# A graph network on one core: GpSimd writes 256 elements of a scratch tile behind every second row gather

## The chip, the core and the metric

The kernel runs on one core of one Trainium2 chip (trn2). A time is the device time of one execution in microseconds (us). A kernel is timed in several runs and the median is given. The profile and the trace are of one execution. PE is TensorE, DVE is VectorE, ACT is ScalarE, POOL is GpSimd and SP is SyncE; the last one only issues DMAs here. The granted clock of PE is a share of its full speed: 0.5 is 1.2 GHz and 1.0 is 2.4 GHz.

## The reference

Eight graphs (b) with 1024 nodes and 128 features go through four layers. A residual sum and a layer norm stand behind each of them.

```
x = _layernorm(x + _L0_gnn_ref(adj, x, L0_W, L0_b))                 # sampled neighbours, max
x = _layernorm(x + _L1_gnn_ref(x, adj, L1_W, L1_b, L1_a))           # graph attention
x = _layernorm(x + _L2_gnn_ref(x, adj, L2_W, L2_a))                 # graph attention
x = _layernorm(x + _L3_gnn_ref(x, adj, att_W, W0, b0, W1, b1))      # masked attention, two steps

def _L0_gnn_ref(A, X, W, b):            # the layer that the change is about
    scores = where(A != 0, -arange(N), -inf)
    vals, idx = top_k(scores, 25)       # the first 25 neighbours of every node
    feats = X[idx], where valid, else -inf
    agg = feats.max(axis=2)             # and at least 0 where a node has 25 neighbours or fewer
    return relu(concatenate([X, agg]) @ W + b)
```

## The kernel before, in words

A graph's 1024 nodes are eight tiles t of 128 nodes, one on each partition. Five instruction streams, one for each engine, are written out by hand. They meet at semaphores, and each stream runs its instructions in the order in which they stand. Graph 0 has a start of its own. Then a loop takes two graphs in each pass, and the last two graphs stand behind it.

The 25 neighbours of layer 0 come in two ways. For the first 21 of them (13 in graph 0), DVE lists the rows of x that are wanted (`find_keys`, `find_members`, which ends in `list_rows` at L1171). GpSimd then issues one indirect DMA for each slot k (`gather`, L508). One such gather fetches 128 rows of 512 bytes, one for each partition, into `gathered`, a ring of three tiles. DVE takes the maximum over the slots of a tile (`pool_tile` at L1204 and L1205, for tile 3 in two halves at L1212 and L1217). It then raises `rows_pooled`, which frees the place in the ring. The other slots are picked by matmuls with one-hot matrices (`make_hot` at L1249 on DVE, L563 and L566 on ACT; `pick` at L817 on PE).

All of this is done one graph ahead. While the engines work on graph b, the lists, gathers and picks of graph b+1 are placed between the steps of graph b, by the table `SIDE`. GpSimd does nothing else once its constants are made: it has 8 tiles of 13 gathers and 56 tiles of 21 gathers, 1280 in all. Before each tile it waits for the list of rows (`rows_ready`, for every second tile) and for the free place (`rows_pooled`). In steady state these waits cut a graph's eight tiles into five bursts, of 42, 21, 21, 42 and 42 gathers. Within a burst the gathers follow each other at once. Other lines named below are L917 and L764 on PE (heads of a graph attention layer and the packing of the adjacency bits) and L1277 on DVE (a small step of the layer norm).

Of the kernel before, what the change touches and what calls it, by code (L numbers as in the profile page):

```python
# [11 lines left out]
BF16 = mybir.dt.bfloat16  # L12
# [7 lines left out]
P = 128  # L20
# [9 lines left out]
GATHERED = (21, 21)  # L30
GATHERED_FIRST = 13
LATE = 6
PICKED = (SAMPLES - GATHERED[0], SAMPLES - GATHERED[1])
PICKS = PICKED[0] + PICKED[1]
BY_DVE = (PICKED[0], PICKED[0] + 1)
PICKED_FIRST = SAMPLES - GATHERED_FIRST
# [67 lines left out]
def gathered_up_to(b, t):  # L104

    return sum(gathered_slots(b, i) for i in range(t % RING, t + 1, RING))


def half_and_slot(b, q):
    if isinstance(b, int) and b == 0:  # L110
        return divmod(q, PICKED_FIRST)
    return (0, q) if q < PICKED[0] else (1, q - PICKED[0])

# [7 lines left out]
def late_rows(t):  # L121

    return LATE if t == 7 else 0

# [13 lines left out]
def build_graph_layers(nc, x, adj, w0, b0, w1, b1, a1, w2, a2, watt, w3a, b3a, w3b, b3b, out):  # L138
    B, N, C = x.shape
    T = N // P  # L140
# [12 lines left out]
    with ExitStack() as ctx:  # L153
        def sb(name, shape, dt=F32):
            return ctx.enter_context(nc.sbuf_tensor(name, shape, dt))
# [4 lines left out]
        def signal(name, per, unit=1, ahead=0, first=None):  # L160
            return Signal(ctx, nc, name, per, unit, ahead, first)
# [48 lines left out]
        row_f = sb("row_f", [P, 2, GATHERED[0]])  # L210
        rows = sb("rows", [P, T, GATHERED[0]], U32)
        gathered = sb("gathered", [P, RING, GATHERED[0] * C])
        running = sb("running", [P, T, N // 2], BF16)
        hot = [sb(f"hot{c}", [P, T // CHUNKS, N // 2], F32R) for c in range(CHUNKS)]
        x_parts = [sb(f"x_part{i}", [P, T, C], F32R) for i in range(X_PARTS)]
# [57 lines left out]
        def pick_bank(b, q):  # L273
# [30 lines left out]
        late_ring = (T - 1) % RING  # L304
        rows_gathered = [signal(f"rows_gathered{i}", gathered_up_to(1, max(range(i, T, RING))) - (i == late_ring) * LATE, 16,
                                first=ring_tiles(i, T) * GATHERED_FIRST - (i == late_ring) * LATE)
                         for i in range(RING)]
        late_gathered = signal("late_gathered", LATE, 16)
        gathers_begun = ctx.enter_context(nc.semaphore("gathers_begun"))
        loads_begun = ctx.enter_context(nc.semaphore("loads_begun"))  # L310
        rows_pooled = signal("rows_pooled", T)
# [148 lines left out]
        @block.gpsimd  # L460
        def _(pool):
            nc.gpsimd.memset(ident[:, :], 0.0).then_inc(consts, 1)
            nc.gpsimd.memset(pack_w[:, :], 0.0).then_inc(consts, 1)
            nc.gpsimd.memset(minus_one[:, :], -1.0).then_inc(consts, 1)
            nc.gpsimd.iota(group_key_i, pattern=[[-(1 << GROUP), G]], base=G << GROUP,
                           channel_multiplier=0).then_inc(consts, 1)
            pool.wait_ge(consts, 4)
            nc.gpsimd.affine_select(out=ident[:, :], in_=ident[:, :], compare_op=ALU.not_equal, fill=1.0,
                                    base=0, pattern=[[-1, P]], channel_multiplier=1).then_inc(consts, 1)

            for bit in range(GROUP):
                nc.gpsimd.affine_select(out=pack_w[:, 0, 0:GP], in_=pack_w[:, 0, 0:GP], compare_op=ALU.not_equal,
                                        fill=float(1 << bit), base=bit, pattern=[[GROUP, GP]],
                                        channel_multiplier=-1).then_inc(consts, 1)
                pool.wait_ge(consts, 6 + bit)
            for j in range(1, HALF):
                nc.gpsimd.tensor_copy(pack_w[:, j, j * GP:(j + 1) * GP], pack_w[:, 0, 0:GP]).then_inc(consts, 1)
            nc.gpsimd.memset(value_sum[:, C:C + 1], float(N)).then_inc(consts, 1)
            nc.gpsimd.memset(n_nodes[:, :], float(N)).then_inc(consts, 1)

            nc.gpsimd.memset(count_all[:, :], 2.0).then_inc(consts, 1)
            nc.gpsimd.memset(plus_one[:, :], 1.0).then_inc(consts, 1)
            for s in range(PICKED[0]):
                nc.gpsimd.memset(minus_count[:, s:s + 1], -float(wanted(1, s))).then_inc(consts, 1)
            steps = (count_through, 1), (count_rest, -1)
            for k, (table, step) in enumerate(steps):
                nc.gpsimd.memset(table[:, :], 2.0).then_inc(counting, 1)
            pool.wait_ge(counting, 2)
            for k, (table, step) in enumerate(steps):
                nc.gpsimd.affine_select(out=table[:, :], in_=table[:, :], compare_op=ALU.is_gt, fill=0.0, base=0,  # L490
                                        pattern=[[step, P]], channel_multiplier=-step).then_inc(counting, 1)
            pool.wait_ge(counting, 4)
            for k, (table, step) in enumerate(steps):
                nc.gpsimd.affine_select(out=table[:, :], in_=table[:, :], compare_op=ALU.not_equal, fill=1.0, base=0,
                                        pattern=[[step, P]], channel_multiplier=-step).then_inc(consts, 1)

            def gather(b, t):
                if t % 2 == 0:
                    pool.wait_ge(rows_ready.sem, rows_ready.at(b, t // 2 + 1))
                if t >= RING:  # L500
                    pool.wait_ge(rows_pooled.sem, rows_pooled.at(b, t - RING + 1))
                elif not (isinstance(b, int) and b == 0):
                    before = max(range(t, T, RING))
                    pool.wait_ge(rows_pooled.sem, rows_pooled.at(b, before + 1 - T))
                pool.sem_inc(gathers_begun, 1)
                for k in range(gathered_slots(b, t)):
                    late = k >= gathered_slots(b, t) - late_rows(t)
                    (late_gathered if late else rows_gathered[t % RING]).raised_by(pool.indirect_dma_start(  # L508
                        out=gathered[:, t % RING, k * C:(k + 1) * C], out_offset=None, in_=x_rows,
                        in_offset=bass.IndirectOffsetOnAxis(ap=rows[:, t, k:k + 1], axis=0)))  # L510

            for t in range(T):
                gather(0, t)
            with pool.Fori(1, B) as b:
                for t in range(T):
                    gather(b, t)
# [575 lines left out]
        def _(dve):  # L1092
# [88 lines left out]
            def pool_tile(b, slot, t):  # L1181
# [8 lines left out]
                if late and isinstance(b, int) and b == B - 1:  # L1190
# [4 lines left out]
                                                 pool_floor[slot][:, t:t + 1], ALU.mult, ALU.max))  # L1195
                    dve.wait_ge(late_gathered.sem, late_gathered.at(b, LATE))
                    link(nc.vector.tensor_reduce(pooled[:, t, :], rows_of[:, :, n - late:n], AX.X, ALU.max))
# [4 lines left out]
                if late:  # L1202
                    dve.wait_ge(late_gathered.sem, late_gathered.at(b, LATE))
                link(nc.vector.tensor_reduce(pooled[:, t, :], rows_of[:, :, 0:n], AX.X, ALU.max))  # L1204
# [292 lines left out]
```

## Time and profile before

| | before |
|---|---|
| median of 3 runs | 2945.58 us |
| lowest and highest | 2940.02, 2952.21 us |
| span of the profiled execution, first to last instruction | 2892.8 us |
| median less that span | 52.8 us |
| busy: PE, PE weight load | 1713.1, 1233.8 us |
| busy: DVE, ACT, POOL | 1366.6, 937.2, 1263.5 us |
| mean granted clock of PE | 0.773 |

Of the profiled execution the span is known. What lies around it is taken as the 52.8 us between the span and the median. No engine is busy for more than 59% of the span, so the time is set by chains of waits from engine to engine or by something that holds the engines up. A busy time is the sum of what the instructions took, and a gap between two instructions is not in it.

### The profile page before, as it was taken

How to read it: one execution, taken by the hardware profiler on the slowest of the kernel's cores; microseconds unless marked ns; L12 is line 12 of the kernel's file. 1: busy time of each engine (PE TensorE's matmuls, PEld its weight loads, DVE VectorE, ACT ScalarE, POOL GpSimd, SP SyncE). 2: the span in 40 equal slices, each digit the busy share in tenths (PEclk: the TensorE clock that was granted, in tenths of full speed). 3: DMA queues.
4: the chain of work that ended last, by engine and by line, in shares of the span. 5: the costliest groups of instructions: out<-in, count | busy, mean ns of one | idle time of the engine just before them, and what ended most of it. 6: DMA issues, size and time to landing. Idle time of an engine off the chain costs nothing.

```text
span 2892.8 us, 27186 instructions
## 1 busy us (share of the span) xinstructions
PE 1713.1 (59%) x8580; PEld 1233.8 (43%) x8580; DVE 1366.6 (47%) x3417; ACT 937.2 (32%) x1311; POOL 1263.5 (44%) x1310
## 2 busy tenths in 40 slices
PE   1655767535765457664574655656455564756778
PEld 0543554424543245343452434434343343533655
DVE  3663664334743347443464434544354544443642
ACT  1010533323433324233332342223432325223223
POOL 5376344455344453444454443544435444255000
PEclk9987777767887668776697766877678776788789
DMA  4221212222222222222232221222312222121001
GB/s 126 61 74 43 71 51 90 55 77 62 59 77 61 66 62 61 77 71 55 58 85 62 70 77 29 80 70 70 77 38 71 70 69 63 36 67 52 23 15 37
DMA packets 160697, 182.18 MB, mean 63 GB/s; under 512 B 106397, under 2 KB 123690, under 8 KB 160554
## 3 DMA queue, kind: packets, MB, share of 16 engines
q1 hardware_dynamic: 119594, 96.43, 12.2%
q0 software_dynamic: 40960, 83.97, 10.8%
q8 instruction: 74, 1.21, 0.2%
q14 instruction: 69, 0.57, 0.1%
HBM read 155.66 MB, written 4.19 MB: 55 GB/s over the span
## 4 chain that ended last, share of the span: by engine, by line
PE 36%; another core or an unknown queue 24%; issue 18%; DVE 12%; ACT 5%; DVEq 4%; DMA 1%; SPq 1%; ACTq 0%
PE big L917 5%; PE spare L817 5%; PE side L1015 4%; PE big L1032 4%; PE big L986 4%; DVEq L69 3%; PE big L843 2%; PE big L999 2%; DVE probs_t L1327 2%; DVE pooled L1204 1%; PE big L817 1%; PE big L908 1%; PE big L864 1%; ACT adj_less L536 1%
## 5 line engine op out<-in xcount | busy, mean ns | idle before, releaser
L508 POOL DMA_INDIRECT gathered<-in_x_dram,rows x1280 | 1259.0, 984 | 1410.7 <-DVE pooled L1205 616.7
L817 PE MATMUL spare<-hot,x_part 128*128 128x512 f32 x1088 | 305.8, 427 | 86.9 <-issue 58.2
L917 PE MATMUL big<-values,probs_t 128*128 128x129 f32 x1792 | 254.0, 299 | 117.8 <-issue 117.0
L917 PEld LDWEIGHTS big<-values,probs_t 128*128 128x128 f32 x1792 | 241.8, 214 | 130.7 <-issue 125.7
L817 PEld LDWEIGHTS spare<-hot,x_part 128*128 128x128 f32 x1088 | 216.0, 203 | 150.5 <-issue 107.2
L1204 DVE TENSOR_REDUCE pooled<-gathered 128x128 f32<-128x2688 f32 (+1 forms) x56 | 253.0, 4517 | 6.4 <-issue 6.4
L986 PE MATMUL big<-probs_t,values 128*128 128x512 f32 x256 | 132.2, 666 | 160.4 <-issue 152.4
L1393 DVE TENSOR_REDUCE neg_max<-big 128x1 f32<-128x1024 f32 x64 | 78.3, 1223 | 286.2 <-remote 182.8
L1015 PE MATMUL side<-recip_diag,work 128*128 128x128 f32 x1024 | 143.6, 296 | 116.7 <-ACT probs_t L679 54.5
L1015 PEld LDWEIGHTS side<-recip_diag,work 128*128 128x128 f32 x1024 | 134.3, 208 | 146.6 <-issue 120.0
L563 ACT ACTIVATE hot<-running,minus_count 128x2048 fp32r<-128x2048 bf16 x84 | 167.4, 1993 | 58.9 <-remote 58.7
L999 PE MATMUL big<-xt,row_gain 128*128 128x512 f32 x256 | 140.0, 674 | 50.4 <-issue 39.2
L1327 DVE SCALAR_TENSOR_TENSOR probs_t<-row_gain,col_gain,adj_t 128x1024 f32<-128x1024 f32 x128 | 156.2, 1292 | 28.0 <-ACT row_gain L619 20.5
L566 ACT ACTIVATE hot<-hot,plus_one 128x2048 fp32r<-128x2048 f32 x84 | 168.2, 2002 | 2.7
L551 ACT CAST running<-spare 128x512 bf16<-128x512 f32 x92 | 53.8, 585 | 324.8 <-PE spare L784 127.6
L672 ACT ACTIVATE work<-big,neg_max 128x1024 f32<-128x1024 f32 x64 | 71.3, 1114 | 265.4 <-DVE neg_max L1393 193.4
L1373 DVE TENSOR_TENSOR probs_t<-big,best_t 128x512 f32<-128x512 f32 x16 | 11.1, 691 | 297.1 <-PE big L957 257.8
L986 PEld LDWEIGHTS big<-probs_t,values 128*128 128x128 f32 x256 | 52.6, 216 | 222.7 <-issue 213.9
L854 PE MATMUL big<-ident,xs 128*128 128x128 f32 x256 | 55.6, 384 | 150.7 <-DVE xs L1296 90.2
L679 ACT COPY probs_t<-side 128x1024 f32<-128x1024 f32 x64 | 64.2, 1003 | 219.3 <-remote 138.5
L1032 PE MATMUL big<-values,probs_t 128*128 128x128 f32 x1024 | 126.1, 289 | 5.4 <-ACT values L608 5.4
L1261 DVE TENSOR_TENSOR best_t<-best_t,spare 128x512 f32<-128x512 f32 x52 | 35.7, 687 | 195.5 <-remote 148.0
(191 smaller groups left out, 2642.0 us busy)
## 6 DMA issues: line engine op xcount, KB each, us to landing
adj_in<-in_adj_dram SPq DMA_DIRECT2D x128, 512.0 KB
gathered<-in_x_dram,rows POOLq DMA_INDIRECT x1280
xs<-in_x_dram SPq DMA_DIRECT2D x8, 512.0 KB
out_dram<-xs SPq DMA_DIRECT2D x8, 512.0 KB
adj_t<-adj_bf SPq DMA_TRANSPOSE x64
packed_t<-group_bits SPq DMA_TRANSPOSE x28
w_sb<-in_L_gnn_W_dram SPq DMA_DIRECT2D x1, 128.0 KB
w_sb<-in_L_gnn_W_dram SPq DMA_DIRECT2D x2, 64.0 KB
```

What stands on the lines that cost most here:

```text
L69: self.settle()
L508: (late_gathered if late else rows_gathered[t % RING]).raised_by(pool.indirect_dma_start(out=gathered[:, t % RING, k * C:(k + 1) * C], out ...
L563: hot_apart.raised_by(nc.scalar.activation(hot[c][:, :, :], running[:, per * c:per * (c + 1), :], ACT.Abs, bias=minus_count[:, s:s + 1]))
L566: hot_made.raised_by(nc.scalar.activation(hot[c][:, :, :], hot[c][:, :, :].bitcast(F32), ACT.Relu, scale=-1.0, bias=plus_one[:, 0:1]))
L817: last = nc.tensor.matmul(pick_bank(b, q), x_parts[part][:, m, :], hot[c][:, m % per, :], start=(m == 0 and part == 0), stop=(m == T - 1 a ...
L917: last = nc.tensor.matmul(heads[:, t, 0:C + 1], probs_t[:, j, t * P:(t + 1) * P], values[:, j, :], start=False, stop=(j == T - 1), skip_gr ...
L986: last = nc.tensor.matmul(low[:, halves[h]], values[:, m, 0:C], probs_t[:, m, halves[h]], start=(m == 0), stop=(m == T - 1))
L999: nc.tensor.matmul((low, high)[t % 2][:, half], queries[:, t * P:(t + 1) * P], xt[:, half], start=True, stop=False, skip_group_check=True)
L1015: last = nc.tensor.matmul(side_t[:, m, :], work[:, (t - 2) % 3, m * P:(m + 1) * P], recip_diag[:, t % 2, :], start=True, stop=True)
L1032: last = nc.tensor.matmul(low_t[:, t, :], probs_t[:, m, t * P:(t + 1) * P], values[:, m, 0:C], start=(m == 0), stop=(m == T - 1))
L1204: link(nc.vector.tensor_reduce(pooled[:, t, :], rows_of[:, :, 0:n], AX.X, ALU.max))
L1327: gat_probs.raised_by(nc.vector.scalar_tensor_tensor(out=probs_t[:, j, :], in0=row_gain[:, :], scalar=col_gain[:, j:j + 1], in1=adj_t[slot ...
```

## The change

GpSimd's stream gets a memset behind each gather with an odd k: 256 bf16 elements on 32 partitions of a new scratch tile, `pause`, which nothing reads. That is 10 in a tile of 21 gathers and 6 in a tile of 13, 608 in all. The partitions go round in four quarters. The last memset of a tile raises a new semaphore `paused`, and the next tile's first gather waits for it. There is no drain instruction behind a memset.

```
 GATHERED_FIRST = 13
 LATE = 6
+PAUSE = 256
+PAUSED = 2
...
+        pause = sb("pause", [P, -(-GATHERED[0] // (4 * PAUSED)), PAUSE], BF16)
...
+        paused = signal("paused", T)
...
             def gather(b, t):
+                if t or not (isinstance(b, int) and b == 0):
+                    pool.wait_ge(paused.sem, paused.at(b, t))
                 if t % 2 == 0:
                     pool.wait_ge(rows_ready.sem, rows_ready.at(b, t // 2 + 1))
...
                         in_offset=bass.IndirectOffsetOnAxis(ap=rows[:, t, k:k + 1], axis=0)))
+                    if k % PAUSED == PAUSED - 1:
+                        quarter = k // PAUSED % 4 * 32
+                        last = nc.gpsimd.memset(pause[quarter:quarter + 32, k // (4 * PAUSED), :], 0.0)
+                paused.raised_by(last)
```

On GpSimd, at the last tile of graph 0 and the first tile in the loop over the graphs, before the change (names of tiles, the shape, a count, and the semaphores that a row waits for):

```order
L508 DMA gathered<-in_x_dram,rows 128x128 [waits rows_pooled]
L508 DMA gathered<-in_x_dram,rows 128x128 x12
L514 UNCONDITIONAL_BRANCH
L514 ISA
L504 ISA [waits rows_ready]
L508 DMA gathered<-in_x_dram,rows 128x128 [waits rows_pooled]
L508 DMA gathered<-in_x_dram,rows 128x128 x20
```

And the same place with the change:

```order
L519 MEMSET pause 32x256
L514 DMA gathered<-in_x_dram,rows 128x128
L524 UNCONDITIONAL_BRANCH
L524 ISA
L505 ISA [waits paused]
L510 REGISTER_ALU [waits rows_ready]
L514 DMA gathered<-in_x_dram,rows 128x128 [waits rows_pooled]
L514 DMA gathered<-in_x_dram,rows 128x128
L519 MEMSET pause 32x256
L514 DMA gathered<-in_x_dram,rows 128x128 x2
```

Twenty gathers in one piece have become pairs with a memset behind each, and a tile's start has one wait more. The other engines' instructions and their order stay as they were.

## Rows read from the trace of the kernel before

**Rows 1.** The page: the span, and the chain that ended last by engine.
```profile
span 2892.8 us, 27186 instructions
PE 36%; another core or an unknown queue 24%; issue 18%; DVE 12%; ACT 5%; DVEq 4%; DMA 1%; SPq 1%; ACTq 0%
```

**Rows 2.** Timeline of POOL, 1047 to 1074: start, length, instruction, idle before.
```profile
1047.27 0.94 POOL L508 DMA_INDIRECT gathered<-in_x_dram,rows  x1 [9.20 <-DVE pooled L1205]
...
1072.23 0.94 POOL L508 DMA_INDIRECT gathered<-in_x_dram,rows  x1 [0.30 <-issue]
```

**Rows 3.** Timeline of PE in the same burst.
```profile
1043.68 12.72 PE L917 MATMUL big<-values,probs_t 128*128 128x129 f32 x100
...
1061.45 1.29 PE L817 MATMUL spare<-hot,x_part 128*128 128x512 f32 x2 [1.16 <-issue]
...
1075.46 3.05 PE L817 MATMUL spare<-hot,x_part 128*128 128x512 f32 x5 [0.59 <-issue]
```

**Rows 4.** Chain of waits, one pick with no gathers beside it.
```profile
1098.23 3.66 PE spare L817 x16
```

**Rows 5.** Windows: length, busy (count) of PE, PEld, DVE, ACT, POOL; PEclk.
```profile
1047.30:1056.20 8.90, 8.90 (x82) 8.90 (x81) 0.00 (x0) 0.00 (x0) 6.77 (x8) 1.00 0.17 46
1056.20:1073.20 17.00, 7.06 (x19) 3.35 (x19) 0.00 (x0) 0.00 (x0) 13.02 (x14) 0.62 0.20 54
1077.00:1110.00 33.00, 23.62 (x127) 18.94 (x128) 27.65 (x83) 19.53 (x33) 0.00 (x0) 0.74 0.12 37
...
860.00:902.00 42.00, 10.30 (x19) 4.28 (x18) 9.43 (x44) 7.95 (x5) 31.82 (x34) 0.59 0.20 53
...
906.00:930.00 24.00, 22.42 (x173) 20.30 (x172) 12.53 (x11) 13.21 (x14) 0.00 (x0) 1.00 0.26 67
...
1141.50:1171.00 29.50, 19.90 (x65) 11.57 (x64) 7.45 (x6) 8.64 (x11) 22.49 (x24) 0.79 0.34 107
...
115.60:152.30 36.70, 28.93 (x122) 22.60 (x122) 30.43 (x28) 0.00 (x0) 30.30 (x22) 0.95 0.14 36
```

**Rows 6.** The page's DMA queues: that of the gathers.
```profile
q0 software_dynamic: 40960, 83.97, 10.8%
```

**Rows 7.** Windows: one graph's period, then its five bursts of gathers.
```profile
1284.80:1635.80 351.00, 200.04 (x1045) 144.85 (x1044) 166.11 (x426) 122.54 (x166) 162.24 (x168) 0.76 0.25 66
1284.80:1337.00 52.20, 14.27 (x52) 7.04 (x50) 16.25 (x51) 7.44 (x15) 39.67 (x42) 0.64 0.28 75
1366.00:1392.20 26.20, 13.78 (x81) 11.01 (x81) 12.28 (x15) 12.65 (x20) 20.00 (x21) 0.72 0.41 110
1409.00:1435.20 26.20, 9.05 (x55) 7.53 (x53) 11.48 (x49) 4.71 (x9) 19.97 (x21) 0.68 0.21 55
1471.00:1527.00 56.00, 30.01 (x132) 18.93 (x130) 22.97 (x49) 16.20 (x27) 42.79 (x42) 0.82 0.30 88
1553.00:1605.40 52.40, 23.67 (x89) 13.31 (x87) 17.58 (x56) 11.93 (x9) 39.81 (x42) 0.71 0.19 51
```

**Rows 8.** Timeline of POOL at the kernel's start: its memsets.
```profile
0.96 0.53 POOL L463 MEMSET pack_w<- 128x512 bf16 x1
1.43 0.10 POOL L464 MEMSET minus_one<- 128x1 f32 x1
...
4.47 0.19 POOL L487 MEMSET count_through<- 128x128 bf16 x1
4.61 0.20 POOL L487 MEMSET count_rest<- 128x128 bf16 x1
```

**Rows 9.** The instructions on `gathered`: duration in ns min/median/max, first and last start.
```profile
L508 POOL DMA_INDIRECT gathered<-in_x_dram,rows x1280: 938/944/2645, 25.4 to 2674.8; - x183
...
L1193 DVE TENSOR_REDUCE gathered<-gathered x1: 3412/3412/3412, 2710.8 to 2710.8; 128x128 f32<-128x1920 f32 x1
```

**Rows 10.** Timelines of POOL and DVE at 1126, and line L1277 as Rows 9.
```profile
1126.20 2.43 POOL L508 DMA_INDIRECT gathered<-in_x_dram,rows  x1 [0.30 <-issue]
...
1125.83 1.22 DVE L1249 TENSOR_SCALAR hot<-running 128x2048 fp32r<-128x2048 bf16 x1
...
L1277 DVE TENSOR_SCALAR rstd<-spread x32: 170/172/418, 301.0 to 2885.4; 128x8 int32<-128x8 int32 x32
```

## Prediction

> **What bounds the kernel now.** I read the page first. No engine is on the chain that ended last for even half of it: PE has 36% of the span, DVE 12%, ACT 5%. But 24% is put down to an unknown source and 18% to issue, which is time in which an engine waited for nothing that the profile shows [rows 1]. So the question is what holds engines that have nothing to wait for.
>
> The timelines of POOL and PE beside each other show it. A burst of 21 gathers runs from 1047.27 to 1073.17, one every 1.25 us (0.94 us and a gap of 0.30) [rows 2]. When it begins, PE is at full pace: 100 matmuls of L917 in 12.72 us. Some 9 us into the burst this ends. The 16 matmuls of the next pick are spread from 1061.45 to 1078.5, which is 17 us, with gaps called issue between them [rows 3]; with no gathers beside it such a pick takes 3.66 us [rows 4].
>
> The windows put rates to it. I count the instructions of PE, PEld, DVE and ACT in a stretch and divide by its length [rows 5]. The first 8.9 us of this burst have 163, or 18.3 a us. The next 17 us have 38, or 2.2 a us, though these are the same programs on the same tiles. The 33 us after the burst have 371, or 11.2 a us. A double burst has the same shape: 86 in the 42 us from 860, or 2.05 a us, and 370 in the 24 us behind it, or 15.4 a us. DVE and ACT sink together with PE, so it is no single engine's queue or port.
>
> It isn't merely that gathers run, though. From 1141.5 to 1171 they run without a gap and there is no such collapse, but the other engines ask for little there, 4.9 a us. And from 115.6 to 152.3, 22 gathers come one in 1.67 us on average, as DVE holds them up, and the others run at 7.4 a us for 36.7 us [rows 5]. I read this as a **shared bucket**: every instruction and every gather puts something in, it empties at a fixed rate, and when it is full all engines go at what is left over, some 2.2 instructions a us at one gather in 1.25 us. Its size follows from the burst at 1047: 8.9 x (18.3 - 2.2) = 143 instructions; the stretch at 1141.5 gives 29.5 x (4.9 - 2.2) = 80. I take 110. What the bucket is, no row shows.
>
> The Trainium skill (NOTIFIC — the notification-queue block, § 3 Interfaces) says that the block which writes out the engines' records has an internal FIFO, and that a full one can stall an engine. By this rule too, gathers further apart would hold the others up less. No row here shows that block.
>
> **The gathers themselves wait for DVE**, as in [rows 2], where the burst starts once L1205 has freed the ring. They are early: the last gather starts at 2674.8 and DVE begins on its tile at 2710.8, 35 us after it ends [rows 9]. A longer burst is therefore hidden as far as data goes: a double one gets 5 us longer (below), which is within the 35 us.
>
> **What the change costs on POOL.** There are 608 memsets. The nearest rows are memsets of 128 and of 512 bf16 elements on 128 partitions. One of 128 holds the next one off by 4.61 - 4.47 = 0.14 us, one of 512 by 1.43 - 0.96 = 0.47 [rows 8]. In between, 256 come to 0.25 us. Bounds: nothing, if a memset on 32 partitions disappears beside the next gather, in the 0.30 us between two; and 0.55 us, if it brings a second such gap with it (0.25 + 0.30). I take 0.25, as the memsets at the start follow each other with no gap. A pair of gathers then takes 2.75 us in place of 2.50, or 1.375 each. A graph's 80 memsets stretch its five bursts from 213 us (the sum of their windows [rows 7]) to 233.
>
> The wait for `paused` hides behind the tile's last gather: the memset that it waits for stands ahead of that gather, which takes 0.94 us. It would cost its own length if a tile's last instruction were the memset.
>
> **What the change gives.** What a gather puts into the bucket, g (in instructions), is bounded by rows. From 115.6 the bucket never fills: 7.4 a us can exceed the allowed rate by at most 110 / 36.7 = 3.0, so 4.4 a us are allowed at one gather in 1.67 us, against 2.2 at one in 1.25. Hence g x (0.80 - 0.60) is at least 2.2, and g at least 11. The bucket also lets 15.4 a us through for 24 us with no gathers, so g is at least (15.4 - 2.2) x 1.25 = 16.5. On the other side, a gather has 40960 / 1280 = 32 DMA packets [rows 6]; one for one, g would be 32. I take the middle, 25. With gathers 1.375 us apart the allowed rate rises by 25 x (1/1.25 - 1/1.375) = 1.8, to 4.0 a us.
>
> One graph has 2681 such instructions in 351 us; 1110 of them lie in its bursts, 5.2 a us, and 1571 in the other 138 us, 11.4 a us [rows 7]. (Five full buckets and 2.2 x 213 make 1019, near 1110, so the picture holds for a whole graph.) With the change the bursts carry 1110 - 2.2 x 213 + 4.0 x 233 = 1573. The 1108 left take 97 us at 11.4. The period is 233 + 97 = 330 us, 21 less. Seven graphs are gathered for in this way: 7 x 21 = 147 us. **2945.6 - 147 = 2799 us.** Graph 0's start, in which DVE already spaces the gathers, I leave as it is. The bounds of g give 7 x 8.5 = 60 us at 16.5 (2886 us) and 7 x 32 = 222 at 32 (2724 us). A memset of 0.55 us with g = 25 gives bursts of 257 us, which carry 2131 at 5.8 a us, and a period of 305: 322 us less, or 2624. A memset that adds nothing gives nothing.
>
> **The port.** A gather that meets a `make_hot` on DVE takes 2.43 us in place of 0.94, and L1277 takes up to 0.418 in place of 0.172 [rows 10]. So the two engines shut each other out. If each of the 608 memsets held a DVE instruction up by 0.25 us, with DVE 12% of the chain, that would be 608 x 0.25 x 0.12 = 18 us. But the median of L1277 is within 2 ns of its minimum, so most of its instructions meet nothing, and I charge nothing.
>
> [...]
>
> **Rivals.**
> - *The stall lasts as long as the burst does.* If gathers at any pace near this one hold the engines to the same count, the bursts are 20 us longer per graph and carry no more: 7 x 20 = 140 us more, 3086. For it: the stall in [rows 5] ends only behind the burst. Against it: the 36.7 us at one gather in 1.67 us. It decides when the allowed rate rises by less than 0.8 a us, which is g below 11. With a short memset it is a smaller loss, 2960 and up.
> - *The pause isn't one.* The memset runs beside the next gather, spacing stays 1.25 us, and nothing changes: 2946. For it: only 32 of 128 partitions are written, the gap of 0.30 us is longer than 0.25, and nothing waits for the memset but the next tile. Against it: gathers and memsets are in one engine's order. The same result would come if only a profiled execution stalled; but the profiled span is not above the median.
> - *A quarter of a pause.* If only the memsets on one of the four quarters hold the gathers up, a pair takes 0.06 us more, the allowed rate rises by 25 x (1/1.25 - 1/1.28) = 0.5, and 218 us of bursts carry 1230; the other 1451 take 127 us. That is 6 us a graph, 40 in all: 2906. The Trainium skill (GPSIMD Engine Reference, § 2.1 Instruction dispatch) says that each of GpSimd's cores has partitions of its own and goes on as soon as its share is done; by this rule, that is what a memset with no wait behind it would do. No row here shows the cores apart.
> - *A rhythm broken for good.* One gather of 2.43 us early in a burst [rows 10] was followed by a double burst with no collapse for 45 us. If a short break does the same, the bursts run freely: 2681 / 11.4 = 235 us of work a graph, of which dependencies would let little more than a fifth of the period be saved, 7 x 45 = 315 us, 2630.
>
> **Chances.** The forecast with its bounds for g: 0.48. The broken rhythm or the long pause: 0.12. A quarter of a pause: 0.10. No change: 0.13. The stall gets longer: 0.17. A measurement here tells a difference of about 0.5% (15 us) from none. So faster is 0.70, same 0.13, slower 0.17. The range goes from 2640 to 2965: it takes in both bounds of g, nearly all of the long pause, and the case of no change, and leaves out the longer stall. The likeliest case by itself is 2724 to 2886.
>
> **What the profile would show.** The 21 gathers of a tile take 28 to 29 us in place of 25.9. In a single burst like that at 1047 the others get 4 instructions a us behind the first 10 us, in place of 2.2, and the 16 matmuls of L817 take under 12 us in place of 17. The stretches between bursts keep 11 a us. I am wrong if the spacing stays 1.25 us, if it grows and the count per burst doesn't, or if g is far from 25.

## The result, and the profile after

| | before | after |
|---|---|---|
| median of 4 runs each | 2945.78 us | 2786.33 us |
| lowest and highest | 2940.02, 2952.21 us | 2771.25, 2793.63 us |
| span of the profiled execution | 2892.8 us | 2782.5 us |

The ratio is 0.9451, with a 95% interval from 0.9419 to 0.9482: 159 us less, where 147 were foretold. The profiled execution of after took 2784.28 us with its 2782.5 us of span. So what lies around a span is 1.8 us. The 52.8 us of before were therefore not something around its span, as the prediction took them. Its profiled execution took some 50 us less than the median, and less than any of the four timed ones. Why isn't on record, nor on which chip it ran: the same kernel has medians of 2902.59 and 2909.38 us on two chips of later series, and 2938.01 and 2951.08 us on two others. The two profiles differ by 110 us only.

The page of after: span, the chain that ended last by engine, and the group of the memsets with its busy time, the mean ns of one, and the idle time before it.

```profile
span 2782.5 us, 27770 instructions
another core or an unknown queue 32%; PE 25%; DVE 16%; issue 11%; ACT 8%; DVEq 6%; DMA 1%; SPq 0%; ACTq 0%
L519 POOL MEMSET pause<- 32x256 bf16 x608 | 195.4, 321 | 24.4
```

The unknown source and issue still have 43% of the chain, against 42% in [rows 1]. The stall is smaller, not gone. A memset takes 0.32 us on average. The timeline of POOL after shows what it adds to the gathers.

```profile
1310.04 0.95 POOL L514 DMA_INDIRECT gathered<-in_x_dram,rows  x1 [0.30 <-issue]
1311.03 0.30 POOL L519 MEMSET pause<- 32x256 bf16 x1
1311.49 0.95 POOL L514 DMA_INDIRECT gathered<-in_x_dram,rows  x1 [0.16 <-issue]
1312.75 0.95 POOL L514 DMA_INDIRECT gathered<-in_x_dram,rows  x1 [0.30 <-issue]
```

Two gathers take 1312.75 - 1310.04 = 2.71 us, where [rows 2] have 2 x 1.25. The 21 gathers of a tile that nothing disturbs take 28.0 us.

Windows of after, in the form of [rows 5]. The first is a stretch of graph 0's start, the next three are a burst of 42 gathers and what follows it, the last is one graph.

```profile
40.00:75.00 35.00, 20.97 (x77) 13.37 (x75) 24.59 (x80) 8.48 (x15) 29.03 (x34) 0.76 0.53 132
1309.00:1334.00 25.00, 24.28 (x177) 22.28 (x178) 22.39 (x38) 16.03 (x22) 20.96 (x25) 0.93 0.44 106
1334.00:1368.00 34.00, 15.69 (x44) 8.23 (x43) 1.68 (x4) 1.35 (x2) 27.63 (x38) 0.60 0.18 48
1372.00:1400.00 28.00, 19.41 (x107) 14.98 (x108) 23.33 (x77) 18.00 (x31) 0.00 (x0) 0.76 0.14 38
1228.20:1573.20 345.00, 207.12 (x1030) 149.56 (x1035) 165.47 (x424) 122.76 (x166) 191.15 (x248) 0.76 0.25 67
```

Counted as in the prediction, PE, PEld, DVE and ACT together: 415 instructions in the first 25 us of the burst, 16.6 a us. Then 93 in 34 us, 2.7 a us. Behind the burst 323 in 28 us, 11.5 a us. A graph has 2655 of them in 345 us; [rows 7] have 2681 in 351. So the fall comes 25 us into this burst, where it came 9 us into that of [rows 5], and it is nearly as deep as the 2.2 of before. A graph of after has four bursts of 42 gathers: the two single ones have joined. The same stretch of the start in the kernel before:

```profile
40.00:75.00 35.00, 8.77 (x18) 1.70 (x18) 6.28 (x31) 3.57 (x7) 26.01 (x28) 1.00 0.19 51
```

That is 74 instructions against 247 of after: a stall, in a place where the prediction saw none. PE in the collapse of the burst at 1309:

```profile
1319.12 14.02 PE L927 MATMUL big<-values,probs_t 128*128 128x129 f32 x108
...
1347.49 3.86 PE L827 MATMUL spare<-hot,x_part 128*128 128x512 f32 x7 [1.00 <-issue]
1351.75 0.40 PE L827 MATMUL spare<-hot,x_part 128*128 128x512 f32 x1 [0.40 <-issue]
1352.47 0.40 PE L827 MATMUL spare<-hot,x_part 128*128 128x512 f32 x1 [0.33 <-issue]
1353.87 0.39 PE L827 MATMUL spare<-hot,x_part 128*128 128x512 f32 x1 [1.00 <-issue]
...
1360.95 0.58 PE L827 MATMUL spare<-hot,x_part 128*128 128x512 f32 x1 [1.60 <-issue]
```

The reader sees 108 matmuls without a gap, and then single ones. The pick at L827 takes 1347.5 to 1361.5, which is 14 us.

Where the 110 us between the two profiles lie, by the first gather of each graph: from graph 0 to graph 1, 173.2 us in place of 203.7 (31 us less). The next six graphs, 343.1 us each in place of 353.5 (62 less). From the first gather for the last graph to the end, 526 in place of 543 (17 less).

### The profile page after: what moved, and what is told of

It is laid out like the page before. It is cut to its first block, busy times and chain, and to the rows that moved or that the text cites. A ratio compares the mean times of both kernels' runs of the same rounds, so it can differ in the third digit from the quotient of the medians.

```text
span 2782.5 us, 27770 instructions
## 1 busy us (share of the span) xinstructions
PE 1692.2 (61%) x8533; PEld 1235.0 (44%) x8580; DVE 1366.5 (49%) x3417; ACT 937.5 (34%) x1311; POOL 1484.2 (53%) x1918
## 3 DMA queue, kind: packets, MB, share of 16 engines
q8 instruction: 74, 1.21, 0.2%
## 4 chain that ended last, share of the span: by engine, by line
another core or an unknown queue 32%; PE 25%; DVE 16%; issue 11%; ACT 8%; DVEq 6%; DMA 1%; SPq 0%; ACTq 0%
DVEq L71 4%; PE side L1025 4%; PE big L1042 2%; PE big L1009 2%; PE spare L827 2%; DVE probs_t L1337 2%; PE big L996 2%; DVE pooled L1214 2%; ACT hot L573 2%; PE big L827 1%; DVE stats L1276 1%; ACT adj_less L546 1%; PE big L927 1%; PE big L864 1%
## 5 line engine op out<-in xcount | busy, mean ns | idle before, releaser
L514 POOL DMA_INDIRECT gathered<-in_x_dram,rows x1280 | 1284.3, 1003 | 1061.6 <-DVE pooled L1215 437.0
L827 PE MATMUL spare<-hot,x_part 128*128 128x512 f32 x1088 | 310.9, 433 | 52.2 <-issue 41.0
L827 PEld LDWEIGHTS spare<-hot,x_part 128*128 128x128 f32 x1088 | 219.4, 207 | 121.3 <-issue 77.8
L927 PE MATMUL big<-values,probs_t 128*128 128x129 f32 x1792 | 233.4, 291 | 16.4 <-issue 15.9
L927 PEld LDWEIGHTS big<-values,probs_t 128*128 128x128 f32 x1792 | 224.8, 205 | 25.5 <-issue 20.6
L1025 PEld LDWEIGHTS side<-recip_diag,work 128*128 128x128 f32 x1024 | 140.2, 217 | 184.3 <-issue 180.2
L519 POOL MEMSET pause<- 32x256 bf16 x608 | 195.4, 321 | 24.4
L1337 DVE SCALAR_TENSOR_TENSOR probs_t<-row_gain,col_gain,adj_t 128x1024 f32<-128x1024 f32 x128 | 154.5, 1279 | 29.5 <-ACT row_gain L629 23.3
L1042 PEld LDWEIGHTS big<-values,probs_t 128*128 128x128 f32 x1024 | 127.8, 209 | 61.1 <-ACT values L618 61.1
L864 PEld LDWEIGHTS big<-ident,xs 128*128 128x128 f32 x256 | 42.1, 193 | 246.5 <-DVE xs L1306 222.4
L853 PE MATMUL big<-w_sb,xt 128*128 128x128 f32 x384 | 81.6, 361 | 104.2 <-issue 87.0
```

Source lines behind the costliest of these rows:

```text
L519: last = nc.gpsimd.memset(pause[quarter:quarter + 32, k // (4 * PAUSED), :], 0.0)
L827: last = nc.tensor.matmul(pick_bank(b, q), x_parts[part][:, m, :], hot[c][:, m % per, :], start=(m == 0 and part == 0), stop=(m == T - 1 a ...
L864: last = nc.tensor.transpose(low[:, t * P:(t + 1) * P], xs[slot][:, t, :], ident[:, :])
L927: last = nc.tensor.matmul(heads[:, t, 0:C + 1], probs_t[:, j, t * P:(t + 1) * P], values[:, j, :], start=False, stop=(j == T - 1), skip_gr ...
L1025: last = nc.tensor.matmul(side_t[:, m, :], work[:, (t - 2) % 3, m * P:(m + 1) * P], recip_diag[:, t % 2, :], start=True, stop=True)
L1042: last = nc.tensor.matmul(low_t[:, t, :], probs_t[:, m, t * P:(t + 1) * P], values[:, m, 0:C], start=(m == 0), stop=(m == T - 1))
```

## The experiments

All ratios are to the kernel before, run on the same chip in the same series; the series ran on different chips, so small differences between ratios of two series are to be read with care. "Spacing" is that of the gathers within a tile: the time of the shortest tile of 21 gathers in the profile, less the last gather's 0.94 us, over 20. "A graph" is the mean of six periods from the first gather of a graph to that of the next.

| run | behind the gathers | spacing, us | a graph, us | ratio (95% interval) |
|---|---|---|---|---|
| before | nothing | 1.25 | 353.5 | 1 |
| e1_short | 2 elements, every second | 1.25 | 363.0 | 1.0047 (1.0012 to 1.0082) |
| the change | 256, every second | 1.35 | 343.1 | 0.9451 (0.9419 to 0.9482) |
| e3_one_gap | 2 x 1280, once in a tile | 1.36 | 337.8 | 0.9488 (0.9449 to 0.9526) |
| e7_four64 | 4 x 64, every second | 1.40 | 315.2 | 0.8982 (0.8955 to 0.9008) |
| e9_each192 | 192, each | 1.40 | 298.5 | 0.8471 (0.8424 to 0.8517) |
| e5_384 | 384, every second | 1.40 | 302.1 | 0.8640 (0.8611 to 0.8669) |
| e8_each256 | 256, each | 1.45 | 262.3 | 0.7696 (0.7672 to 0.7719) |
| e2_double | 512, every second | 1.46 | 280.4 | 0.7980 (0.7919 to 0.8041) |
| e10_drain | a drain, every second | 2.29 | 400.1 | 1.1097 (1.1043 to 1.1150) |

Longer memsets of 1024 elements, and a single one of 2560 in a tile, have no result: their scratch tile does not fit in SBUF beside the others. So nothing is measured between 1.46 and 2.29 us.

### Presence or length: 2 and 512 elements

```diff
-PAUSE = 256
+PAUSE = 2        # the other run: 512
```

> The memsets write 2 elements in place of 256; their number, their places and the wait for `paused` stay. Theory A (what helps is the time that a memset puts between gathers): a memset of one element per partition took 0.10 us at the kernel's start, against a spacing of 0.21 us that 256 elements add; a pair of gathers should take 2.55 to 2.60 us, and a third of the gain of 159 us is left, about 2890 us. Theory B (what helps is that the row of gathers is broken at all, by a memset or by the wait for `paused`): 2786 us, whatever the length. If even a short memset adds as much as a long one, a pair stays at 2.71 us and the run can't tell them apart; the spacing is to be read first.

> The memsets write 512 elements. Theory A: the time of a memset doubles, a pair takes 2.92 us instead of 2.71 and a tile of 21 gathers 30.1 us instead of 28.0. Each 0.21 us in a pair was worth 159 us at first; the second should be worth less, as part of the stall is gone: 60 to 100 us, so 2690 to 2730 us, with the fall of the others' pace put off beyond the 25 us of now. Theory B: 2786 us. Theory C (the gathers are soon late): the slack of 28 us before DVE takes the last tile shrinks to some 12 us, and does not decide yet; if it does, 2800 to 2830 us.

Two elements left the spacing as it was (a tile takes 26.0 us) and gained nothing; the ratio is a little above 1. So neither the memset's presence nor the wait for `paused` gains anything. 512 elements gave 2355 us, a far larger gain than any of the theories expected. The second 0.21 us in a pair of gathers was worth some 430 us more where the first was worth 159. The windows of the version with 512 elements, on the same work as the burst at 1309:

```profile
1402.00:1430.00 28.00, 28.00 (x200) 25.95 (x199) 22.20 (x36) 14.29 (x21) 23.50 (x27) 0.94 0.40 97
1430.00:1466.00 36.00, 22.36 (x102) 16.59 (x101) 26.67 (x81) 19.76 (x33) 30.00 (x34) 0.75 0.24 66
```

16.3 instructions a us in the first 28 us, and 8.8 in the other 36: no collapse within 42 gathers. The 8.8 is what the engines asked for, as PE waits 11.8 us for DVE (L1306) at the start of that window. Theory C falls too, as the last tile of each graph from graph 1 on still has 11 us or more of slack.

### The same length in one piece, and 384 elements

```diff
-                    if k % PAUSED == PAUSED - 1:
-                        quarter = k // PAUSED % 4 * 32
-                        last = nc.gpsimd.memset(pause[quarter:quarter + 32, k // (4 * PAUSED), :], 0.0)
+                    if k == 9:
+                        for piece in range(2):
+                            last = nc.gpsimd.memset(
+                                pause[piece * 32:piece * 32 + 32, 0:gathered_slots(b, t) // 4 * PAUSE], 0.0)
```

The tile `pause` is made wider for it. The other run has PAUSE = 384 and is else the change.

> The same elements written as with the change, but in two memsets of 1280 elements, one right behind the other, after the tenth gather of a tile (2 x 768 in graph 0). A tile's gathers take 28.0 us as with the change, with one gap of some 2.1 us. What two runs have shown: no pause, a fall after 9 us; 256 elements (a gather in 1.355 us), after 25 us; 512 (1.46 us), never. Theory D (a critical spacing): a store is left behind by gathers and filled at 1/spacing less 1/c; 9 us and 25 us give c = 1.42 us and a store of 0.87 gather. A gap of 2.1 us then empties the store, each tile has some 8 us of stall in place of 17, and the time is about 2680 us. Theory A (only the mean spacing counts): 2786 us. Theory E (a stall, once begun, lasts until well behind the last gather, as a recovery takes 3.5 us without gathers): 2900 us or more.

> The memsets write 384 elements: a gather in 1.41 us. Theory D (critical spacing 1.42 us, store 0.87 gather): the stall sets in only after some 100 us of gathers without a break, so it is all but gone: 2350 to 2450 us. A gradual law (what the others may do rises with the spacing step by step): midway between the 2786 us of 256 and the 2355 us of 512 elements, 2570 us.

One gap gave the same as ten small ones, 0.949 against 0.945, so theory E falls and theory A holds here. The timeline of POOL and then five windows show how it works.

```profile
297.17 2.35 POOL L519 MEMSET pause<- 32x1280 bf16 x2
299.68 1.18 POOL L514 DMA_INDIRECT gathered<-in_x_dram,rows  x1 [0.16 <-POOL pause L519]
```

```profile
285.00:299.00 14.00, 11.92 (x70) 10.02 (x70) 11.96 (x15) 13.90 (x22) 11.18 (x12) 0.82 0.55 109
300.00:310.00 10.00, 9.99 (x71) 9.89 (x71) 9.29 (x19) 0.98 (x1) 7.56 (x9) 0.79 0.27 86
310.00:326.00 16.00, 5.51 (x18) 3.76 (x17) 0.99 (x2) 0.00 (x0) 12.30 (x14) 0.64 0.20 53
328.40:331.40 3.00, 1.62 (x7) 1.79 (x7) 0.00 (x0) 0.00 (x0) 2.37 (x3) 0.50 0.14 36
331.40:341.90 10.50, 4.38 (x13) 3.26 (x13) 0.00 (x0) 0.00 (x0) 8.03 (x9) 0.50 0.21 54
```

The first gap of this burst, 2.5 us between two gathers, is followed by some 10 us at full pace (162 instructions from 300 to 310, 16.2 a us). Then come 2.3 a us until the second gap, from 325.9 to 328.4. That one, after 16 us of stall, brings back little: 14 instructions in 3 us (4.7 a us), then 2.5 a us, while PE has matmuls of L928 to do. So about 10 us at full pace is what a gap gave at best.

This corrects a reading of mine. In the burst of after at 1309 three gathers were long. They lie beside eight instructions of DVE's L1337 (a step of a graph attention layer), whose row stands behind theirs:

```profile
1314.20 1.91 POOL L514 DMA_INDIRECT gathered<-in_x_dram,rows  x1 [0.16 <-issue]
...
1317.87 1.83 POOL L514 DMA_INDIRECT gathered<-in_x_dram,rows  x1 [0.16 <-issue]
...
1321.46 1.83 POOL L514 DMA_INDIRECT gathered<-in_x_dram,rows  x1 [0.16 <-issue]
```

```profile
1312.81 9.66 DVE L1337 SCALAR_TENSOR_TENSOR probs_t<-row_gain,col_gain,adj_t 128x1024 f32<-128x1024 f32 x8 [1.51 <-issue]
```

The last of them ends 14 us into the burst. If such a gather, like the gap, gives relief, then a good part of the 25 us without a stall is theirs, and 11 us only are to be set against the 9 us of before. The burst at 1047 of before had no such gather.

A pair of bursts without any long gather shows what the spacing alone does. They stand at the same place of a graph, at 849.6 in before and at 1148.5 in after. Windows of before, then of after:

```profile
849.60:864.60 15.00, 13.56 (x67) 8.33 (x65) 12.22 (x27) 3.12 (x4) 11.42 (x12) 1.00 0.18 50
864.60:885.60 21.00, 0.00 (x0) 0.00 (x0) 3.42 (x20) 0.00 (x0) 16.01 (x17) 0.53 0.20 53
```

```profile
1148.50:1163.50 15.00, 13.62 (x68) 8.34 (x65) 12.56 (x28) 3.12 (x4) 12.39 (x16) 1.00 0.17 45
1163.50:1184.50 21.00, 14.48 (x40) 7.84 (x40) 4.88 (x29) 9.41 (x6) 16.90 (x23) 0.91 0.18 48
1184.50:1205.40 20.90, 3.10 (x11) 2.35 (x10) 0.00 (x0) 0.60 (x1) 17.14 (x24) 0.50 0.18 49
```

The first 15 us are alike, with 163 and 165 instructions. In the next 21 us before has 20 (1.0 a us) and after has 115 (5.5 a us). Then after has 22 in 20.9 us, 1.1 a us. So 0.1 us more between the gathers puts the fall off by some 15 to 20 us, without any long gather, and the pace behind it is as low as before.

384 elements gave 0.864, so 2545 us if before takes 2946. The gradual law had 2570 and is right; theory D (a sharp critical spacing of 1.42 us) had 2450 at most and falls. Its two numbers were the 9 and the 25 us that I have just taken apart. The windows of this version:

```profile
876.00:903.00 27.00, 26.37 (x209) 24.01 (x208) 23.27 (x38) 16.66 (x22) 22.45 (x28) 1.00 0.40 101
903.00:936.00 33.00, 12.30 (x31) 6.65 (x31) 14.58 (x67) 10.50 (x16) 27.14 (x35) 0.64 0.21 51
```

The rate in the second part is 145 / 33 = 4.4 a us. With the 2.2, the 2.7 and the 8.8 above, which come from different pieces of work, what the engines do behind the first part of a burst rises with the spacing slowly at first (1.25, 1.35), then steeply (1.40, 1.46).

### More instructions for the same elements

```diff
-                        last = nc.gpsimd.memset(pause[quarter:quarter + 32, k // (4 * PAUSED), :], 0.0)
+                        for piece in range(4):
+                            last = nc.gpsimd.memset(
+                                pause[quarter:quarter + 32, k // (4 * PAUSED), piece * 64:piece * 64 + 64], 0.0)
```

> Each memset of 256 elements is written as four of 64, with 1824 instructions more on GpSimd. 2 elements added 0.02 us to a pair of gathers, so a pair should keep 2.71 us, or get up to 0.1 us longer. Theory F (what overflows is a count in which every instruction has a part, so that three more in each 2.71 us, against some 18 a us of the others at their best, hasten it): slower than 2786 us, 2830 or so. Theories A and D (spacing alone): 2786 us, and less if a pair gets longer than 2.75 us.

It was faster than the change, at 0.898. The four memsets take 0.40 us together, which makes the spacing 1.40. It lies between the ratios at 1.35 and at 1.40, so spacing explains its sign, and theory F's loss didn't come. But it stays 0.034 above 384 elements, on the same chip, with a spacing that is only 0.007 us less (1.397 against 1.404). From 1.354 to 1.404 us the ratio falls by 0.081, so 0.007 us are worth about 0.01 (an estimate). At this slope the other 0.02 is not explained by the mean spacing. That the 1824 instructions cost it is possible, but not shown.

### Even gaps

```diff
-PAUSED = 2
+PAUSED = 1      # 256 elements in one run, PAUSE = 192 in the other
```

> A memset of 256 elements behind every gather in place of 512 elements behind every second: the mean spacing is that of 512 (1.46 us), but every gap is alike (0.51 us), where 512 elements gave 0.30 and 0.72 us in turn. Theories A and D: 2355 us within 30 us. Rival G (a gap of some 0.7 us is what lets something drain, and one of 0.5 us isn't enough): 2700 us or more.

> A memset of 192 elements behind every gather: a gather in some 1.40 us, all gaps alike, the mean of 384 elements behind every second (1.41 us, ratio 0.864 to the kernel before). If only the mean spacing counts: ratio 0.86 to 0.87. If even gaps are worth more (at a mean of 1.46 us they gave 0.770 against 0.798): about 0.83. If the room that a graph's gathers took in the version with 256 behind each (GpSimd holds 77% of the chain there) is now what counts, and the stall stays away: below 0.77.

Rival G falls: gaps of 0.5 us are enough. Even gaps are somewhat better than uneven ones of the same mean, 0.770 against 0.798 at 1.46 us and 0.847 against 0.864 at 1.40. The second pair is close: it ran on two chips, and in microseconds it is 2489 against 2507. With 256 elements behind each gather the kernel takes 2235 us where the one before takes 2903, and the page tells what bounds it now: the chain by engine, and the group of DVE's maxima.

```profile
POOL 77%; issue 14%; PE 6%; DVE 1%; ACT 1%; SPq 0%; POOLq 0%; DMA 0%; DVEq 0%; ACTq 0%
L1214 DVE TENSOR_REDUCE pooled<-gathered 128x128 f32<-128x2688 f32 (+1 forms) x56 | 252.7, 4512 | 372.7 <-DMA gathered<-in_x_dram,rows 370.1
```

DVE waits 370 us for gathers, so this is the other end: 336 gathers follow each other with no gap above 1.5 us, and a graph takes the 262 us that its gathers do. The stall is away, in windows as busy as any:

```profile
1036.00:1064.00 28.00, 28.00 (x195) 24.53 (x194) 24.87 (x47) 19.06 (x23) 24.06 (x34) 0.92 0.39 97
1075.00:1117.00 42.00, 34.31 (x224) 27.89 (x225) 33.76 (x93) 19.89 (x34) 36.18 (x52) 0.88 0.34 79
```

459 and 576 instructions are 16.4 and 13.7 a us.

### A drain in place of the memset

```diff
-                        last = nc.gpsimd.memset(pause[quarter:quarter + 32, k // (4 * PAUSED), :], 0.0)
+                        last = nc.gpsimd.drain()
```

The tile `pause` is gone with the memsets.

> A drain instruction of GpSimd behind every second gather, in place of the memset: nothing is written. No run shows what it adds to a pair of gathers: at least nothing (2 elements added 0.02 us), at most what a gather takes to finish once it has been begun, 0.94 us. If time between gathers is all that counts, the ratio lies on the line of the runs with a memset: 1.00 at 1.25 us a gather, 0.945 at 1.355, 0.864 at 1.41, 0.80 at 1.46. If it is the write to the scratch tile that helps, the ratio stays 1.00 whatever the spacing.

My upper bound for a drain, 0.94 us, was far too low. A drain adds 2.2 us, and all the others wait for GpSimd:

```profile
999.42 0.94 POOL L513 DMA_INDIRECT gathered<-in_x_dram,rows  x1 [2.59 <-issue]
1000.66 0.94 POOL L513 DMA_INDIRECT gathered<-in_x_dram,rows  x1 [0.30 <-issue]
1004.07 0.94 POOL L513 DMA_INDIRECT gathered<-in_x_dram,rows  x1 [2.46 <-issue]
```

The group of DVE's maxima on the same version's page:

```profile
L1212 DVE TENSOR_REDUCE pooled<-gathered 128x128 f32<-128x2688 f32 (+1 forms) x56 | 250.2, 4467 | 1235.2 <-DMA gathered<-in_x_dram,rows 1233.6
```

So it can't tell whether a pause that writes nothing helps; it tells what too much of it costs. The 8 tiles of a graph take 8 x 50 = 400 us.

### Graph 0 alone

```diff
-                    if k % PAUSED == PAUSED - 1:
+                    if isinstance(b, int) and k % PAUSED == PAUSED - 1:
...
```

The waits for `paused` and its raising are kept for graph 0 alone as well.

> The memsets of 256 elements stand in graph 0's 8 tiles alone, and the loop's gathers follow each other as before. What the profiled executions put into the start (203.7 us to the first gather of the loop before, 173.2 with the change) is a gain by itself: -31 us, ratio 0.989. If that gain is lost again in the loop, as graph 1 then waits for what it would have waited for anyway: 1.00.

The ratio is 0.9906 (0.9872 to 0.9940), and its start takes 170 us: the 34 us between the medians fit the 31 us that the profiles gave the start, and they are kept. Its other graphs, with gathers as in the kernel before, take 362.0 us each. So do those of e1_short (363.0) and of e12_half_row (362.3). The profiled execution of before with its 353.5 was the odd one, by 9 us a graph, which makes up the 50 us by which it was below the median.

### Bytes and rows

```diff
+    x_halves = x.rearrange("b n (h c) -> (b n h) c", h=2)
...
-                        out=gathered[:, t % RING, k * C:(k + 1) * C], out_offset=None, in_=x_rows,
+                        out=gathered[:, t % RING, k * C:k * C + C // 2], out_offset=None, in_=x_halves,
```

This run and the next two also clear the ring `gathered` once ahead of the first gather.

> The kernel before, whose gathers fetch 64 of a row's 128 elements (and from rows of half the number, so the output is another); half the bytes, the same number of gathers and of rows in each, no memset between them. If what holds the engines up is the writing of each gather's descriptors, or anything else that goes by the number of gathers or rows: ratio 1.00 within 0.01, with the fall of the others' pace after 9 us of a burst. If it is the bytes that GpSimd's gathers move past the other engines: half of the bytes is more relief than spacing gave, 0.80 or less.

The ratio is 1.0009 (0.9974 to 1.0044), with the stall where it was. Two windows of its burst at 675:

```profile
675.00:684.50 9.50, 9.50 (x62) 7.69 (x61) 7.83 (x12) 9.14 (x19) 7.31 (x8) 1.00 0.22 41
684.50:701.00 16.50, 3.12 (x11) 2.34 (x10) 7.94 (x16) 6.90 (x4) 12.54 (x14) 0.53 0.45 112
```

154 instructions in 9.5 us, and 41 in the next 16.5 (2.5 a us). So the bytes have no part in it.

```diff
-                        out=gathered[:, t % RING, k * C:(k + 1) * C], out_offset=None, in_=x_rows,
-                        in_offset=bass.IndirectOffsetOnAxis(ap=rows[:, t, k:k + 1], axis=0)))
+                        out=gathered[0:64, t % RING, k * C:(k + 1) * C], out_offset=None, in_=x_rows,
+                        in_offset=bass.IndirectOffsetOnAxis(ap=rows[0:64, t, k:k + 1], axis=0)))
```

> The kernel before, each gather of which fetches the rows of 64 nodes in place of 128 (half of the maxima are then over other values, so the output is another); as many gathers, no memset between them. If what fills up goes by the number of gathers: the stall is as it was or, where a gather of 64 rows is shorter (0.5 us and a gap of 0.30, say, so that one comes in 0.8 us), deeper during a burst, which is then shorter; the others' pace still falls some way into a burst. If it goes by the rows (or what is written for each): the spacing at which nothing fills up, 1.43 us for 128 rows, is 0.71 us for 64. Gathers in 0.8 us then never hold anyone up, and as GpSimd has time to spare, the ratio is at or below the 0.77 that 256 elements behind each gather gave. If a gather of 64 rows still takes 1.25 us, by the gathers 1.00, by the rows 0.77 or less.

This run told something else. On its chip the kernel before itself took 1909.89 us (13 runs, 1903.98 to 1914.29), and this one 1899.06: ratio 0.9947 (0.9928 to 0.9967). The other four series had 2902.6 to 2951.1 us for the same kernel. On this chip there is no stall to be seen, with gathers as close as ever. POOL's timeline of the 64-row version:

```profile
1163.10 0.90 POOL L509 DMA_INDIRECT gathered<-in_x_dram,rows  x1 [0.30 <-issue]
1164.31 0.90 POOL L509 DMA_INDIRECT gathered<-in_x_dram,rows  x1 [0.30 <-issue]
```

A window of the same profile, all but unbroken gathers, and the chain of its page by engine:

```profile
1012.00:1168.00 156.00, 134.58 (x796) 103.42 (x794) 120.29 (x326) 89.86 (x118) 116.41 (x126) 0.91 0.31 77
```

```profile
PE 41%; DVE 24%; POOL 10%; issue 10%; DVEq 8%; ACT 6%; DMA 2%; SPq 0%; POOLq 0%; ACTq 0%
```

126 gathers, one in 1.21 us within a tile and in 1.24 on average, and beside them 2034 instructions in 156 us, 13.0 a us. The unknown source is gone from the chain, and a graph takes 217 us. The last run joined both questions: 64 rows and the memsets.

> The change with gathers of 64 rows in place of 128 (half of the maxima are over other values, so the output is another): a memset of 256 elements behind every second gather. A pair should take 2.42 + 0.21 = 2.63 us, a tile 27.2 us. The chip of the last run was one on which the kernel before took 1910 us and no stall stood in the trace, where three chips ahead of it took 2903 to 2951 us; there 64 rows were worth 0.5%. So what to expect goes by what the kernel before takes in this run. If some 2940 us and what fills up goes by the number of gathers: on the line of the runs with 128 rows (1.00 at 1.25 us, 0.945 at 1.355 us), 0.96 to 0.97 at 1.315 us. If some 2940 us and it goes by the rows: the stall is gone, and a graph takes the 218 us of its gathers plus a few us: 0.70 or below. If some 1910 us: the memsets cost what they add to the gathers, as GpSimd is on the chain there: 8 x 1.5 = 12 us in a graph, 7 graphs, less what slack hides; ratio 1.02 to 1.04.

Its chip had the stall (before: 2909.38 us). The ratio is 0.9739 (0.9700 to 0.9777) at a spacing of 1.31 us, near the 0.96 to 0.97 that the number of gathers gives, and far from the 0.70 of the rows. Its collapse is as deep as before's: 57 instructions in 29 us, as PE's count of 29 and DVE's of 0 show.

```profile
990.00:1018.00 28.00, 25.90 (x171) 23.52 (x170) 22.90 (x38) 15.53 (x22) 23.16 (x29) 0.87 0.32 79
1018.00:1047.00 29.00, 13.06 (x29) 6.03 (x28) 0.00 (x0) 0.00 (x0) 23.44 (x34) 0.50 0.11 25
```

One thing these runs do not part. The row of the gathers' DMA queue on the page of the half-row run (packets, MB, share):

```profile
q0 software_dynamic: 40960, 42.02, 7.5%
```

The MB are half of those in [rows 6], but the packets are as many, 32 a gather, and both runs with 64 rows have the same packets and MB. So what fills up may go by the gathers or by their DMA packets.

What the change does on a chip without the stall wasn't measured. GpSimd has 10% of the chain there, and a graph's eight tiles would take 8 x 28 = 224 us where a graph takes 217, so a loss is to be expected (an estimate), and a large one with 256 elements behind each gather (262 us a graph).

## Why the prediction was right, and where its steps were off

- **The mechanism** is right: close gathers stall all engines, and room between them gives time back. e1_short and the runs at 1.40 and 1.46 us show it in both directions. The rivals fall. The pause is a real one: a tile takes 28.0 us. A stall as long as the burst would have cost time. A quarter of a pause would show one gap in four, but in all four quarters the gathers on both sides of a memset start 1.45 us apart (median), where 1.25 is the spacing without one. No 45 us of free running follow a break, about 10 us do at best.
- **The price of a memset**: 0.21 us in place of 0.25, and 28.0 us for a tile, at the lower end of the 28 to 29 foretold. `paused` cost nothing, as e1_short shows.
- **The slack** of the last tile: 28 us or more are left of 35 in the graphs from 1 on.
- **The step that failed is g**, what a gather puts in, "I take the middle, 25", with its linear law. It gave 4.0 instructions a us behind the first 10 us of a burst. Behind the fall 2.7 and 1.1 were measured, and the pick takes 14 us where I gave it under 12. What the bursts gained instead is a later fall: in the bursts at 849.6 and 1148.5 with their like work 115 instructions in place of 20 in the 21 us behind the first 15, then the same low pace as before. In the burst at 1309 the fall came after 25 us in place of 9, and long gathers that the new timing brought may have a part in that. Carried further, the law is wrong by a factor: at 1.46 us it gives 2.2 + 25 x (1/1.25 - 1/1.46) = 5.1 a us, where 8.8 to 13.7 ran. The evidence for a large store from the stretch at 1141.5 was misread as well. Two long gathers stand ahead of it, one of them at 1126 in [rows 10].
- **"Graph 0's start ... I leave as it is"** was wrong, and worth 31 us. I had looked at 115.6 to 152.3, where DVE spaces the gathers. From 40 to 75 nothing does, and the engines had 74 instructions there.
- **The sum**: 7 x 21 = 147. By the two profiles a graph gains 10.4 us. Against the 362 us that three other profiled kernels with unspaced gathers took, it is 19 us, close to the 21, and 7 x 19 with the 31 of the start would make 164, near the 159 measured. So the predicted time was hit by a rate that was too high, a missing delay of the fall, and a missing start that make up for each other. That it came within 13 us is luck, and its range, 2640 to 2965, took in the case of no change as well.
- **The port**: charged with nothing, and nothing in the runs asks for more. Gathers were stretched beside DVE at 1314 to 1321 (1.83 and 1.91 us); the instruction beside them is L1337, which the prediction did not name. Whether that helped or hurt isn't shown.
- **The profiled span as an argument**: the prediction held against a stall in profiled executions alone that the profiled span is not above the median. That shows nothing, as the timed executions of the series have a span of their instructions on record like the profiled ones, 1.7 to 2.0 us below their times. None here is known to have run without such a record.

The Trainium skill (NOTIFIC — the notification-queue block, § 3 Interfaces) says that an internal FIFO of that block which fills can stall an engine. By this rule spaced gathers would be a relief, and the runs agree in direction. No run here shows that block, nor why one chip has no stall, so it stays a conjecture.

Open: what it is that fills up by the number of gathers or of their packets, whether the other engines' instructions have a part in it (16.4 a us for 28 us fill nothing at 1.45 us), and what is different about the one chip. Open too is the rival that the recording of the instructions takes part in the stall. If it does, the gain would be less where nothing is recorded.

## What to carry to other kernels

When all engines slow down together and the profile names only issue or an unknown source, look at what one engine issues back to back, and try spacing it before touching the engines that wait. Try more than one length: here the first 0.1 us a gather gave 5%, the second 15 to 18% more, and at 2.3 us it was a loss, and an even gap behind each instruction did best. Measure on more than one chip, and without the profiler where you can, before keeping it, since such a pause buys nothing where the stall isn't there.

## What the runs showed of the hardware

- A drain on GpSimd behind an indirect DMA costs 2.2 us, ten times a memset of 32 x 256 elements (0.30 us busy, 0.21 us in the spacing), while a memset of 2 elements vanishes beside the next gather.
- Two chips of one kind differ by a factor of 1.54 (2946 against 1910 us) on the same kernel. The one trace from the quick chip, with gathers of 64 rows, has no stall; that the whole factor comes from it is not shown.
- In the stall, PE's instructions start on a grid: the L827 matmuls above at 1351.75, 1352.47 and 1353.87, 0.72 and 1.40 us apart. In e12_half_row one kind of matmul follows the other at 2.1 us:

```profile
690.85 0.38 PE L921 MATMUL big<-values,probs_t 128*128 128x129 f32 x1 [1.74 <-issue]
692.95 0.38 PE L921 MATMUL big<-values,probs_t 128*128 128x129 f32 x1 [1.72 <-issue]
694.39 0.37 PE L921 MATMUL big<-values,probs_t 128*128 128x129 f32 x1 [1.06 <-issue]
696.51 0.38 PE L921 MATMUL big<-values,probs_t 128*128 128x129 f32 x1 [1.76 <-issue]
```

These steps of 2.10, 1.44 and 2.12 us are three, two and three times 0.7 us.
